# Attention kernel on 8 cores: score matmuls issued in pairs of units, a one-instruction eviction of the masked expert values, and a later tanh

## The reference, cut to what matters

```python
xn = layernorm(x)                        # x: 8 x 4096 x 1024, one batch element per core
Q, K, V = xn @ Wq, xn @ Wk, xn @ Wv      # 16 heads of 64
alpha = softmax(Q @ K.T / 8)             # over ALL keys
s = where(causal, alpha, 0) @ V          # masked after the softmax: the row sum keeps every key
# the gate
logits = normalize(xn) @ normalize(sim) - sigmoid(gates)      # 8 experts
m  = logits > 0 (at least the top 2)     # token x expert mask
rw = softmax over the chosen experts
q, k, v = [sum_e m[:, e] * (xn @ P[e]) for P in (q_proj, k_proj, v_proj)]   # width 128
a = causal_softmax(q @ k.T / sqrt(128)) @ v
f = sum_e (m * rw)[:, e] * (a @ o_proj[e])
out = x + s * silu(f)
```

## Time and profile before

| | us |
|---|---|
| median of 3 runs | 2438.66 |
| lowest, highest | 2414.32, 2522.07 |
| the profiled execution, its own time | 2416.78 |
| its span, slowest core (0) | 2415.2 |
| spans of the 8 cores | 2407.9 to 2415.2 |
| busy in that span: PE, ACT, DVE, POOL | 2115.4, 2101.2, 1511.3, 217.0 |

### The profile page before, as it was taken

One profiled execution on the slowest core, in us unless ns is written; L12 is line 12 of the kernel. 1 busy time (PEld: TensorE's weight loads), 2 busy tenths in 40 slices (PEclk: granted clock), 3 DMA queues, 4 the chain that ended last, 5 costly groups with the idle time before them and its releaser, 6 DMA issues.

```text
span 2415.2 us, 67224 instructions; the slowest of 8 cores (2407.9 to 2415.2 us)
## 1 busy us (share of the span) xinstructions
PE 2115.4 (88%) x22982; PEld 1059.0 (44%) x22982; DVE 1511.3 (63%) x5775; ACT 2101.2 (87%) x2296; POOL 217.0 (9%) x272
## 2 busy tenths in 40 slices
PE   3999999999999999999888888888888888787886
PEld 2644544455445544455334433334344554333332
DVE  5656766666666666666555655555544444788886
ACT  3799999899998999999988888888899999777786
POOL 0110000000000000000100000000100000222222
PEclk9969999999999999999999999999999999999998
DMA  7571011101010000000400000000200001454543
GB/s 186 126 71 21 16 20 17 19 15 19 17 23 21 15 19 17 20 15 11 45 10 4 6 8 11 10 4 10 41 9 6 4 7 51 137 179 137 182 166 117
DMA packets 108967, 109.41 MB, mean 45 GB/s; under 512 B 84832, under 2 KB 89184, under 8 KB 108640
## 3 DMA queue, kind: packets, MB, share of 16 engines
q1 hardware_dynamic: 57568, 90.43, 12.2%
q0 software_dynamic: 51072, 14.68, 6.1%
HBM read 95.46 MB, written 24.31 MB: 50 GB/s over the span
## 4 chain that ended last, share of the span: by engine, by line
PE 67%; issue 11%; DVE 10%; ACT 9%; DVEq 2%; DMA 1%; ACTq 0%; POOL 0%; POOLq 0%; SPq 0%
PE RG L746 21%; PE PVB L788 13%; PE FB L821 8%; ACT EB L1204 8%; PE FB L852 5%; PE FB L858 5%; PE FB L828 4%; PE FB L854 4%; PE FB L868 3%; DVE XM L1100 3%; DVE EB L1015 2%; PE RG L727 1%; DVE KTa L1109 1%; ACT XM L1180 1%; PE RG L702 1%
## 5 line engine op out<-in xcount | busy, mean ns | idle before, releaser
L1204 ACT ACTIVATE EB<-RG 128x1024 bf16<-128x1024 f32 (+4 forms) x2184 | 2014.8, 1049 | 173.8 <-PE RG L746 148.7
L1015 DVE SCALAR_TENSOR_TENSOR EB<-EB 128x256 bf16<-128x256 bf16 (+3 forms) x2176 | 819.8, 423 | 202.5 <-ACT EB L1204 200.6
L821 PE MATMUL FB<-xnT,WS 128*128 128x512 bf16 x896 | 278.5, 391 | 43.7 <-DVE EW L1100 17.3
L852 PE MATMUL FB<-XM,EW 128*128 128x256 bf16 x1024 | 254.7, 275 | 3.3 <-issue 3.3
L854 PE MATMUL FB<-XM,EW 128*128 128x256 bf16 x1024 | 252.2, 272 | 0.0
L788 PE MATMUL PVB<-VAa,EB 128*128 128x65 bf16 (+1 forms) x4224 | 235.0, 197 | 19.4 <-DVE AO L1036 14.9
L746 PE MATMUL RG<-KTb,QT 64*128 64x512 bf16 (+3 forms) x1088 | 200.8, 375 | 42.5 <-ACT EB L1204 42.2
L788 PEld LDWEIGHTS PVB<-VAa,EB 128*128 128x128 bf16 x4224 | 174.9, 100 | 140.9 <-issue 140.3
L788 PE MATMUL PVB<-VAb,EB 128*128 128x65 bf16 (+1 forms) x4224 | 231.4, 196 | 3.7 <-ACT EB L1204 1.4
L746 PE MATMUL RG<-QT,KTa 64*128 64x256 bf16 (+1 forms) x2176 | 217.1, 280 | 15.0 <-ACT EB L1204 13.0
L746 PE MATMUL RG<-QT,KTb 64*128 64x256 bf16 (+1 forms) x2176 | 214.6, 277 | 13.0 <-ACT EB L1204 12.8
(11 more groups left out here) (130 smaller groups left out, 1675.3 us busy)
## 6 DMA issues: line engine op xcount, KB each, us to landing
EW<-x SPq DMA_DIRECT2D x58, 512.0 KB, 6.4
XM<-wT SPq DMA_DIRECT2D x32, 512.0 KB, 3.9
out<-EW SPq DMA_DIRECT2D x26, 512.0 KB, 5.0
MB<-mT SPq DMA_DIRECT2D x16, 512.0 KB, 4.0
s_sp<-S SPq DMA_DIRECT2D x112, 64.0 KB, 1.7
KF<-s_sp SPq DMA_DIRECT2D x32, 224.0 KB, 2.7
KF<-x SPq DMA_DIRECT2D x6, 512.0 KB, 7.5
out<-KF SPq DMA_DIRECT2D x6, 512.0 KB, 4.1
```

The lines of the kernel that those rows point to most:

```text
L821: mm = e.matmul(s.FB[:, 0:512], s.WS[:, col * 1024 + x * 128:col * 1024 + x * 128 + 128], s.xnT[:, x * 4096 + g.n * 512:x * 4096 + g.n * 5 ...
L852: e.matmul(s.FB[:, 0:256], s.EW[:, c0:c0 + 128], mv, start=(x == 0), stop=(x == 63), skip_group_check=True)
L1015: op = e.scalar_tensor_tensor(a, a, 1.0, b, ALU.mult, ALU.add, accum_out=s.PART[:, col:col + 1])
L1204: e.activation(s.unit_cols(u, s.eb(u)), s.unit_cols(u, s.RG[u % 3][:, :]), AF.Exp, scale=(SC_FFN if x.kind == "F" else SC_MAIN)).then_inc( ...
```

## The change

- `tensor_prog` goes in **batches** of two steps: scores of b and b+1 back to back, then the value matmuls of the batch, then its fill. `place_pv` and `pace` round steps down to even ones. The wait before both scores is `a_ex >= b - 1` (exp of unit b-2 is done). `pace` puts at most 5 quanta in a batch, starts a group at the earliest in the batch after the one in which the last ended, and paces pair 7 at 0.90 of a block instead of 0.84.
- The E groups of pairs 0 to 3 are 3, 5, 4, 4.
- A Y group is evicted by one VectorE multiplication of 512 columns (PSUM by the broadcast mask) into `yt`, two f32 buffers in `XM`; GpSimd sums the eight parts of both groups in three additions of 512, 256 and 128 columns with drains (item `vsum`, 32 times). The ones of `vfa` are set by GpSimd.
- Keys are moved; tanh k goes from 1.7 to 3.9 steps behind the end of its group, and the items behind it (gate, sg, add1, the final f) by about as much.

Core of the diff:

```diff
@@ pair_groups @@
-        ffn = [Group("E", 0, b) for b in range(2)]
+        ffn = [Group("E", 0, b) for b in range(3)]
...
-        b0 = (2, 7, 12, 16)
+        b0 = (3, 8, 12, 16)
@@ place_pv, place_fill, pace @@
-                self.pvs.setdefault(t, []).append((u, key, x == 0, x + 1 == len(lst)))
-            self.block_end[key] = t
+                self.pvs.setdefault(t - t % 2, []).append((u, key, x == 0, x + 1 == len(lst)))
+            self.block_end[key] = t - t % 2
...
-                    self.pace(q, [], b0, b1, 0.84, wt, cap=4)
+                    self.pace(q, [], b0, b1, 0.90, wt)
-    def pace(self, q, a, s0, s1, part, wt, cap=3):
+    def pace(self, q, a, s0, s1, part, wt, cap=5):
...
-            n_here = 0
+            n_here = len(self.fill[s])
...
-            s += 1
+            s += 2
@@ order_engines @@
-            act.append((u + 2.0, "exp", u))
+            act.append((u + 1.0, "exp", u))
-                dve.append((u + 3.0, "red", u))
+                dve.append((u + 2.2, "red", u))
-                pool.append((u + 2.9, "mask", u))
+                pool.append((u + 2.1, "mask", u))
-            dve.append((t + 0.6, "pve", key))
+            dve.append((t + 1.0, "pve", key))
-            dve.append((self.g_end[g] + 0.9, "evac", g))
+            dve.append((self.g_end[g] + 1.9, "evac", g))
+        for t in range(32):
+            pool.append((self.g_end[Group("Y", 0, 2 * t + 1)] + 3.0, "vsum", t))
-            kt = eb + 0.9
-            act.append((kt + 0.8, "tanh", k))
-            dve.append((kt + 2.5, "gate", k))
-            dve.append((kt + 3.6, "sg", k))
-            pool.append((kt + 4.6, "add1", k))
+            kt = eb + 1.9
+            act.append((kt + 2.0, "tanh", k))
+            dve.append((kt + 4.5, "gate", k))
+            dve.append((kt + 5.6, "sg", k))
+            pool.append((kt + 6.6, "add1", k))
-            f = max(fin_t[(7, m)], self.g_end[Group("Z", 7, 8 * m + 7)] + 4.8)
+            f = max(fin_t[(7, m)], self.g_end[Group("Z", 7, 8 * m + 7)] + 8.0)
@@ gpsimd_prog @@
+            elif kind == "vsum":
+                yt = s.yt[y % 2]
...
+                e.wait_ge(sem["v_fe"], PLAN.g_no[Group("Y", 0, 2 * y + 1)] + 1)
+                e.tensor_tensor(yt[:, 0:512], yt[:, 0:512], yt[:, 512:1024], ALU.add)
+                e.drain()
+                e.tensor_tensor(yt[:, 0:256], yt[:, 0:256], yt[:, 256:512], ALU.add)
+                e.drain()
+                e.tensor_tensor(s.vfa[:, y * 130:y * 130 + 128], yt[:, 0:128], yt[:, 128:256], ALU.add
+                                ).then_inc(sem["g_y"], 1)
@@ tensor_prog @@
-        for sidx in range(PLAN.NS):
...
+        for b in range(0, PLAN.NS, 2):
+            here = [u for u in (b, b + 1) if u < PLAN.NU]
...
+            if b >= 2 and here:
+                e.wait_ge(sem["a_ex"], b - 1)
+            for u in here:
+                self.tensor_scores(e, u).then_inc(sem["p_qk"], 1)
@@ tensor_need (pair 6), sync_prog wbl @@
-            need.append(Group("Y", 0, 63))
+            e.wait_ge(sem["g_y"], 32)
@@ vector_evac, Y @@
+            if t >= 2 and half == 0:
+                e.wait_ge(sem["g_y"], t - 1)
+            op = e.tensor_tensor(s.yt[t % 2][:, half * 512:half * 512 + 512].rearrange("p (c d) -> p c d", d=128),
+                                 s.FB[:, 0:512].rearrange("p (c d) -> p c d", d=128),
+                                 bass.AP(s.msk, t * 8 + half * 4, [[256, 128], [1, 4], [0, 128]]), ALU.mult)
```

More of the change, by code:

```diff
@@ L84, in pair_groups @@
     if p == 0:
-        ffn = [Group("E", 0, b) for b in range(2)]
-        return [Group("L", 0, 0)] + nx[:4] + [Group("T", 0, 0)] + nx[4:12] + ffn[:1] + nx[12:16] + ffn[1:] + nx[16:]
+        ffn = [Group("E", 0, b) for b in range(3)]
+        return ([Group("L", 0, 0)] + nx[:6] + [Group("T", 0, 0)] + nx[6:12] + ffn[:1] + nx[12:15] + ffn[1:2]
+                + nx[15:20] + ffn[2:] + nx[20:])
     if p in (1, 2, 3):
-        b0 = (2, 7, 12, 16)
+        b0 = (3, 8, 12, 16)
         ffn = [Group("E", 0, b) for b in range(b0[p - 1], b0[p])]
@@ L155, in place_fill @@
         U = self.units
-        self.fill = {s: [] for s in range(self.NS + 400)}
+        self.fill = {s: [] for s in range(0, self.NS + 400, 2)}
         self.groups = []
@@ L178, in place_fill @@
                         q = q[:4] + [Group("Q", 7, 3)] + q[4:]
-                    self.pace(q, [], b0, b1, 0.84, wt, cap=4)
-        self.NS = max([self.NS] + [s + 1 for s in self.fill if self.fill[s]])
-    def pace(self, q, a, s0, s1, part, wt, cap=3):
+                    self.pace(q, [], b0, b1, 0.90, wt)
+        self.NS = max([self.NS] + [s + 2 for s in self.fill if self.fill[s]])
+    def pace(self, q, a, s0, s1, part, wt, cap=5):
         U = self.units
@@ L186, in pace @@
         q, a = list(q), list(a)
-        cur, done, cum, s = None, 0, 0.0, s0
+        cur, done, cum, s = None, 0, 0.0, s0 + s0 % 2
         while q or a or cur:
-            if s < s1:
-                cum += wt[U[s].kind]
+            for y in (s, s + 1):
+                if y < s1:
+                    cum += wt[U[y].kind]
             goal = total * cum / W
-            n_here = 0
+            n_here = len(self.fill[s])
             while done < goal and n_here < cap:
@@ L232, in order_engines @@
             for m in range(8):
-                t = max(max(self.block_end[(p, m, "M", J)] for J in (15 - m, m)) + 0.7,
-                        self.end_of[(p, m)] + 3.1)
+                t = max(max(self.block_end[(p, m, "M", J)] for J in (15 - m, m)) + 1.1,
+                        self.end_of[(p, m)] + 2.3)
                 fin_t[(p, m)] = t
@@ L635, in tensor_prog @@
         U = PLAN.units
-        for sidx in range(PLAN.NS):
[L637 to L642, removed]
-                self.tensor_scores(e, sidx).then_inc(sem["p_qk"], 1)
-            for u, key, first, end in PLAN.pvs.get(sidx, ()):
+        for b in range(0, PLAN.NS, 2):
+            here = [u for u in (b, b + 1) if u < PLAN.NU]
+            for u in here:
+                if PLAN.first_of[(U[u].p, U[u].m)] == u:
+                    self.tensor_need(e, U[u].p, U[u].m)
+            if b >= 2 and here:
+                e.wait_ge(sem["a_ex"], b - 1)
+            for u in here:
+                self.tensor_scores(e, u).then_inc(sem["p_qk"], 1)
+            for u, key, first, end in PLAN.pvs.get(b, ()):
                 if first and PLAN.block_no[key] >= 1:
@@ L650, in tensor_prog @@
                 self.tensor_pv(e, u, first, end).then_inc(sem["p_pv"], 1)
-            for g, x in PLAN.fill.get(sidx, ()):
+            for g, x in PLAN.fill.get(b, ()):
                 self.tensor_fill(e, g, x)
```

35 lines of the change are left out of this document (10 added, 25 removed).

## The result

The changed kernel takes 2347.32 us (median of 5 runs, 2342.36 the lowest), the kernel before 2417.08 in the same series: ratio 0.970, interval 0.9632 to 0.9767. I had forecast 2265. The direction holds, but of a gain of 152 us against the profiled execution only about 70 came, and the time lies outside the forecast's own range (2210 to 2320), inside the wider one (2180 to 2385). The 80 missing us are what this document looks for. In some executions of every kernel the cores of one die or of both show a lower granted clock and take some per cent longer; the ratios are of the other executions alone, and where fewer than three of those are left I give them one by one.

What follows compares the result with a forecast made beforehand. PE bounds pairs 1 and 2, ACT pairs 0 and 6, a late chain 4 and 5, none full in 7. Start 109, pairs 243, 253, 245, 244, 258, 258, 308, 330, tail 15: 2263 span, 2265 us; range 2210 to 2320.

Steps and rivals of the forecast that it cites:

- the paragraph on the other keys: Part 2, moved keys: order of row sums and evictions priced at nothing, covered by DVE idle of 100 us and more a pair.
- the rival of the hand-over: Some 330 groups hand over FB late, PE's next scores queued behind; 0.6 us more each gives 2463 us; chance 0.06.
- the rival in which it is paid between units too: Row change also paid between a batch's two units, so nothing saved: 2413 us, no change; chance 0.06.
- the 28 us of PE in a pair: Part 1: one 0.21 us row change saved in each of 132 batches, 28 us of PE a pair; bounds 0 and 28.
- the 8 to 13 us of slack: Part 1: loss where PE's sum and ACT's floor are equal, as buffer-wait slack falls from 1.08 to 0.17 us.
- the 25 us for heavy batches: Part 2, pairs 4 and 5: nearly half the batches carry five quanta (1.99 us PE); 25 us added, giving 258 each.
- ACT's 233: ACT's floor from its exponentials in a pair of 264 units: no pair of the changed kernel can be shorter than 233 us.
- The signs: Expected: pairs 1 to 3 at 244 to 253, ACT over 92% busy, Y evictions 0.69 us, pair 7 DVE near 90%.
- signs of being wrong: ACT waits on RG above 0.3 us in most batches, an eviction of 1 us and more, or pair 7 above 350.
- The Y eviction: Part 2, pairs 4 and 5: one 0.69 us operation cuts each 1.16 us stall to some 0.2, saving 30 us a pair.
- the rival of the lock: GpSimd and DVE block each other; held row sums delay FB evictions, pair 7 stays at 360: 2333 us; chance 0.17.
- DVE comes next: Part 4, pair 7: 71 us of ACT waits before tanh go, DVE's 293 us stay; taken 330, bounds 293 and 370.

Runs made afterwards that it cites:

- the same E groups: Kernel with both edits, E groups of pairs 0 to 3 spread as before (2, 5, 5, 4 instead of 3, 5, 4, 4): 2285.72 us, ratio 0.946.
- the wait by unit: Changed kernel, but each unit's scores wait for their own buffer (exponential of u-3) instead of one wait per batch: 2335.89 us, ratio 0.967.
- batches of four: Kernel with both edits, at most four quanta a batch in pairs 0 to 6 instead of five: 2273.86 us, ratio 0.9405.
- kernel without batches: Kernel before with the new Y eviction, the sum on GpSimd and the later tanh: 2345.63 us; with fin also behind the FB eviction 2330.91 us.
- both edits: Changed kernel with fin behind the FB eviction and each unit waiting for its own buffer: 2283.33 us, ratio 0.9444.
- the swap: Changed kernel, with fin put behind the FB eviction wherever it stood directly before it (27 places): 2300.33 us, ratio 0.9518.

## Why the prediction was right and wrong, point by point

**The step that failed** is the paragraph on the other keys: "a row sum or eviction still stands behind exponentials that end before it, so I price that order at nothing; the cover is DVE's idle time". I counted DVE's load and not what stands before the eviction. `fin` is 1.7 us on DVE, and the new keys put it directly ahead of an eviction of `FB` in 27 of 64 places, where it had been 18. Idle time of an engine hides work only where the next item isn't behind it. That order cost 47 us of the 82. I had seen the risk in the rival of the hand-over ("whatever DVE is in"), put it at up to 1.2 us, spread it over 330 groups and gave it 0.06; in truth ACT stood 2.9 to 4.6 us behind it in 13 places of pairs 0 to 6.

**The batches: right in mechanism, too dear in the sum.** The change between 64 and 128 rows is paid once a batch, and the rival in which it is paid between units too falls. But I took the 28 us of PE in a pair whole, and 20 us of pair 1's time for it. With the same E groups and `fin` out of the way, PE's busy time of pair 1 falls by 17 us (256.6 to 239.4, core 4, with the wait by unit) and the pair by 11. Over the kernel the forecast had some 80 us for the batches; they brought 0 as built, 31 with `fin` moved, 48 with the wait by unit too.

**Pairs 1 to 5 with `fin` moved: in part luck.** 254, 247, 247, 256 and 256 against 253, 245, 244, 258 and 258 is not the sum coming true term by term. Pairs 1 and 2 got 4 and 3 us outside the batches (270 and 270 to 267 and 267, medians of the cores), which the sum didn't have. Of the 8 to 13 us of slack that I took for pairs 1 to 3, the wait by unit and batches of four give back 2 to 4 in each. Of the 25 us for heavy batches in pairs 4 and 5 (by the terms given beside it, 56 x 0.2, it would be 11) batches of four give back 2. The rest of what keeps these pairs 11 us and more above ACT's 233 stays open; 4 us of it in pairs 2 and 3 is that ACT itself is busy 237.

**The signs.** ACT's waits were to be short (0.1 to 0.3 us) and many; 77 of them were, 100 were longer. None of the signs of being wrong came: the waits above 0.3 us are 100 in some 960 batches, the eviction is 0.69 us, pair 7 is under 350. They asked for a loss in most batches and couldn't see one in 14 places. PE's idle time behind the Y evictions is 27 us in the two pairs, for 73; I had said under 15.

**The Y eviction: right.** 290 and 290 fall to 262 and 263 in the kernel without batches (I took 30 us off each). The cost of GpSimd's sums came as in the rival of the lock, but DVE's room hid most: 3 and 5 us. That rival's 2333 us is the nearest to the measured time, by luck: its 38 us in pairs 4 and 5 were 8, and what pair 7 pays for the lock it paid before as well (the row sum's mean is 0.633 us for 0.636).

**Pair 6.** I had 308; it took 316, with `fin` moved too, and 311 with the wait by unit (313 on core 4). ACT was at its floor and had nothing to lose but slack: here I took too little.

**Pair 7: right that DVE comes next, 6 us too short (10 on core 4).** 71 us of ACT's waits before tanh fell to 26 and the pair by 20, since DVE had 293 of 360 before and kept 288. 5 of the us missing are `fin`. The rule I cited (the Trainium skill, SBUF — State Buffer, section Who interferes with whom) bears out: 1.89 and 2.11 us beside each other. In pair 7 of the kernel with both edits 39 row sums of 256 columns start while GpSimd adds; each ends 0.28 us or more behind the addition, and they take 1.57 us in the mean, where those with no addition beside them take 0.43. The 10 copies out of `FB` that start so take 0.68 us, like the others. I priced the removal of the lock nowhere, as the change doesn't remove it; it is the largest thing left.

**Tail: 15 taken, 21 measured.** The last evictions also stand behind a `fin`:

```profile
2318.58 0.28 DVE L1065 TENSOR_REDUCE cs<-PART 128x4 f32<-128x32 f32 x2
...
2320.20 0.68 DVE L1115 COPY KTa<-FB 128x512 f32<-128x512 f32 x1
...
2321.25 3.57 PE L886 MATMUL FB<-EW,XM 128*128 128x512 bf16 x8 [3.34 <-DVE KTa L1115]
```

PE stands 3.34 us and then runs eight quanta in 3.57 us where eight take 1.7 at the full clock (the granted clock from 2321 to 2325 is 0.50); the tail is 19 with the swap.

**Sum.** 82 us are missing: 47 are `fin`. Of the 35 left (2300 against 2265), by medians of the cores, pair 0 has 11, pair 6 8, pairs 1 to 3 7 together, the tail 4 and pair 7 1, less 3 in pairs 4 and 5; some 7 are that the slowest core is that much over the others. The wait by unit and batches of four bring 26 us (2274), but part of them I had charged, so they don't explain the 35. In pair 0 the extra E group is worth 6 us (10 on core 4), where I had counted 14 and let ACT's floor hide most; what else the pair's start at a granted clock of 0.93 to 0.94 costs in batches was not tried and stays open. One sum of the prediction doesn't follow from its words: the rival of a change paid between units too adds 6 x 23 + 10, where 28 in each of six pairs less 13 and 10 more give 165, so 2430; "no change" stands.

## What to carry to other kernels

Where one bank is handed over between engines, list what stands ahead of the handing item in the second engine's order, and how long it takes; the load of that engine says nothing on it (here it was busy 66% and cost 47 us). An item that nobody waits for goes behind it. Where several engines are near full, look at the fullest one's busy time: in pair 7 here 1 us less of DVE gave 0.7 us in one kernel and 1.0 in another, and a second engine that blocks it adds to that busy time.

## What the runs showed that I had not expected

- A stall of PE can cost twice. Behind the stall of 3.14 us that ends at 818.44 (core 4, changed kernel) the granted clock is 0.50 for some 3 us, and in the tail 0.50 until the end. It isn't so behind every one: behind the stall of 3.01 us shown above it is 1.00, and four quanta take 1.02 us. In pairs 4 and 5 the granted clock is 0.98 and 0.97 in the changed kernel and 1.00 with the swap, in pair 1 0.98 and 0.99.
- The swap of `fin` and copy is worth three times as much with batches (47 us) as without (15). The changed order has 27 such places for 18, and its places are worse ones; each stall of PE's fill now holds the scores of two units. Which of these counts how much was not tried.
- A row sum that starts 0.05 us after GpSimd's addition takes 2.11 us, longer than the addition (1.89): it waits for all of it and ends 0.27 us behind it.
